# Clustering setup of a two-layer image kernel: loads issued in the stage before, entry ahead of the last stores, fewer and wider operations

## The chip, the cores and the metric

The kernel is one program on one core of a Trainium2 chip. The metric is the device time of one execution in microseconds (us). The runs of the kernel before took a median of 7005.86 us.

## What is computed

The input is x of shape (2, 96, 256, 256) in float32. Layer 0 adds to it a window attention followed by an MLP with a depthwise convolution, on the group-normalised x. Layer 1 adds a clustering step to the result, which is called x1 in the kernel:

```
x = x + L0(_gn(x))          # attention windows, fc1, 5x5 depthwise conv, fc2
x = x + L1(_gn(x))          # clustering
# L1, for y = _gn(x), 2 images, 4 heads of 24 channels, each image folded into 4 quarters
feat  = f_w y + f_b ;  value = v_w y + v_b
centres, value_centres = 2 x 2 average pooling of feat and of value, for each quarter
sim   = sigmoid(beta + alpha * <unit(centre), unit(feat)>), kept for the best centre alone
agg   = (sim @ value + value_centres) / (sum(sim) + 1)
out   = proj_w (agg @ sim) + proj_b
```

Because everything ahead of the similarity is linear in x once the group statistics are known, the kernel folds the normalisation, both projections, and the product with the centres into one weight matrix for each quarter, called `rhs` (97 rows: 96 channels and one row for the biases; 208 columns: feature, value and 16 dot products). The stage that builds it is the setup of the clustering.

## The kernel before, in words

The program is a row of stages, each a block of instruction streams, one stream for each engine, with a barrier of all engines at its end: statistics, attention, `fc1`, `conv`, `fc2`, `cluster_setup`, `cluster`. The change touches `fc2` and `cluster_setup`, and the call of both in `program`.

`fc2` is the second product of the MLP. It goes over 14 tiles of rows (2 halves each). SyncE and ScalarE issue its DMAs (SP and ACT queues): x tiles `f_xa` (L1346), convolution results `f_sa` and `f_sbb` (L1356, L1357) into two buffers each. TensorE multiplies (L1411, L1414), VectorE adds the product and the bias onto `f_xa` (L1431) and takes sums for the pooling (L1437), and ScalarE takes sums of squares (L1449). Each tile of x1 is then stored (L1368) on both queues, and both streams end with a wait until all stores have landed (L1391 on SyncE). GpSimd has no stream here.

`cluster_setup` begins when those waits are over. SyncE issues 18 small loads of weights and constants (L1561), GpSimd sets four tiles (L1565 to L1569), and TensorE waits for all 18 loads and for the folded sums. VectorE leads one chain: fold the sums (L1623, L1625), gather them with TensorE (L1585), statistics, a square root on ScalarE (L1575), the scaled weights `wfv` (L1648), means `xm` (L1651, after which `stage` is 4), centres (L1595 to L1661). Then it spreads the centres and the means by quarter and head: 32 times two operations of 4 columns, `ctr` (L1668) and `xmq` (L1669). TensorE multiplies them (L1601, L1606), and VectorE writes 8 times two parts of `rhs` (L1674, L1675) and four copies of `value_centres` (L1678). Every VectorE operation here is followed by a wait on its own semaphore, in the helper

```
def link(ins):
    n[0] += 1
    ins.then_inc(dch, 1)
    dve.wait_ge(dch, n[0])
```

`cluster` follows: its loads of x1 start (L1776, L1781), VectorE sets tiles (L1937 to L1939), and TensorE's products with `rhs` (L1821) begin.

Of the kernel before, what the change touches and what calls it, by code (L numbers as in the profile page):

```python
# [7 lines left out]
F32 = mybir.dt.float32  # L8
BF16 = mybir.dt.bfloat16
ALU = mybir.AluOpType  # L10
# [1296 lines left out]
def fc2(nc, p, xs, sdr, x1, tab):  # L1307
# [5 lines left out]
    with ExitStack() as ctx:  # L1313
# [13 lines left out]
        psum = ctx.enter_context(nc.psum_tensor("f2_ps", [128, 2 * CGRP, 512], F32))  # L1327
# [6 lines left out]
        block = ctx.enter_context(nc.Block())  # L1334
# [37 lines left out]
        def _(sp):  # L1372
# [17 lines left out]
            for u in range(XA):  # L1390
                sp.wait_ge(stored[u], 16 * XLOADS * len(range(u, NTILE, XA)))  # L1391
# [49 lines left out]
        def _(act):  # L1441
# [24 lines left out]
            for u in range(XA):  # L1466
                act.wait_ge(stored[u], 16 * XLOADS * len(range(u, NTILE, XA)))
# [3 lines left out]
NCTR = 4  # L1471
# [3 lines left out]
NFC = 2 * C + EM  # L1475

# [26 lines left out]
def cluster_setup(nc, p, tab, t):  # L1503


    with ExitStack() as ctx:
        def sb(name, shape, dt=F32):
            return ctx.enter_context(nc.sbuf_tensor("cs_" + name, shape, dt))

        NBK = 16  # L1510
        folded = sb("folded", [128, CGRP, NBK + 1])
        pick = sb("pick", [128, B, 32])
        bsum = sb("bsum", [C, B, NBK])
        stat = sb("stat", [C, 2, B])
        avg = sb("avg", [C, 2, B])
        sq = sb("sq", [C, B])
        sd = sb("sd", [C, B])
        eps = sb("eps", [C, 1])
        scale = sb("scale", [C + 1, B])
        shift = sb("shift", [C, B])  # L1520
        group = sb("group", [C, C])
        heads = sb("heads", [C, CH_HEADS])
        same = sb("same", [C, C])
        fv_t = sb("fv_t", [C, 2 * C])
        fv_b = sb("fv_b", [C + 1, 2 * C])
        f_col = sb("f_col", [C, 1])
        f_nat = sb("f_nat", [C, B, C + 1])
        alpha = sb("alpha", [C, 1])
        wfv = sb("wfv", [C + 1, B, 2 * C])
        xm = sb("xm", [C + 1, B, NBK])  # L1530
        xmq = sb("xmq", [C + 1, NREG, CH_HEADS, NCTR])
        cf = sb("cf", [C, B, NBK])
        cs = sb("cs", [C, B, NBK])
        cn = sb("cn", [C, B, NBK])
        ctr = sb("ctr", [C, NREG, CH_HEADS, NCTR])
        psum = ctx.enter_context(nc.psum_tensor("cs_ps", [128, 8, 512], F32))
        loaded = ctx.enter_context(nc.semaphore("cs_loaded"))
        ones_set = ctx.enter_context(nc.semaphore("cs_ones_set"))
# [5 lines left out]
        gathered = ctx.enter_context(nc.semaphore("cs_gathered"))  # L1544
        block = ctx.enter_context(nc.Block())
        loads = [(pick[:], p["k_pick"]), (group[:], p["k_group"]), (heads[:], p["k_heads"]), (same[:], p["k_same_head"]),
                 (fv_t[:, 0:C], p["f_wt"]), (fv_t[:, C:], p["v_wt"]),
                 (fv_b[C:C + 1, 0:C], p["f_b"].rearrange("(a c) -> a c", a=1)),
                 (fv_b[C:C + 1, C:], p["v_b"].rearrange("(a c) -> a c", a=1)),
                 (f_col[:], p["f_b"].rearrange("(c a) -> c a", a=1)),  # L1550
                 (f_nat[:, 0, 0:C], p["f_w"]), (f_nat[:, 1, 0:C], p["f_w"]),
                 (alpha[:], p["sim_alpha"].partition_broadcast(C)),
                 (t["beta"][:], p["sim_beta"].partition_broadcast(128)),
                 (t["eye"][:], p["k_eye"]), (t["proj"][:], p["proj_wt"]),
                 (t["proj_b"][:], p["proj_b"].rearrange("(c a) -> c a", a=1)), (t["own_channels"][:], p["k_own_channels"]),
                 (t["combine"][:], p["k_combine"])]

        @block.sync
        def _(sp):
            for to, of in loads:  # L1560
                sp.dma_start(to, of).then_inc(loaded, 16)  # L1561

        @block.gpsimd
        def _(pool):
            pool.memset(eps[:], 1e-5).then_inc(ones_set, 1)  # L1565
            pool.memset(scale[C:C + 1, :], 1.0).then_inc(ones_set, 1)
            pool.memset(xm[C:C + 1, :, :], 1.0).then_inc(ones_set, 1)
            pool.wait_ge(ones_set, 3)
            pool.memset(t["value_centres"][:], 0.0).then_inc(ones_set, 1)  # L1569

        @block.scalar
        def _(act):
            act.wait_ge(ones_set, 4)
            act.wait_ge(stage, 2)
            act.activation(sd[:], sq[:], ACT.Sqrt, bias=eps[:]).then_inc(ach, 1)  # L1575
            act.wait_ge(pch, 4)
            act.activation(cs[:].rearrange("p b n -> p (b n)"), psum[0:C, 4, 0:B * NBK], ACT.Sqrt).then_inc(ach, 1)

        @block.tensor
        def _(pe):  # L1580
            pe.wait_ge(loaded, 16 * len(loads))
# [29 lines left out]
        def _(dve):  # L1611
# [7 lines left out]
            def staged():  # L1619
                dve.sem_inc(stage, 1)  # L1620
# [24 lines left out]
            dve.wait_ge(loaded, 16 * len(loads))  # L1645
# [457 lines left out]
```

## Time and profile before

| what | us |
|---|---|
| median of 3 runs | 7005.86 (7005.22 to 7007.62) |
| the profiled execution, its own time | 6989.15 |
| its span, first to last instruction | 6987.4 |
| `fc2`, from its first load to the end of its stores | 5363.5 to about 6056.8 |
| `cluster_setup`, first instruction to the last VectorE copy | 6057.2 to 6103.1 |
| `cluster`, from its first load to the end | 6103.6 to 6987.4 |

Times inside the execution are counted from its first instruction. "Busy" is the time in which an engine had an instruction running; PEclk is the granted clock of TensorE as a share of its full 2.4 GHz; the DMA share is the mean busy share of the core's 16 DMA engines. The execution that was profiled was 16.7 us shorter than the median of the runs.

### The profile page before, as it was taken

What the parts mean: (1) busy time and instruction counts of PE and PEld (TensorE: products, weight loads), DVE (VectorE), ACT (ScalarE), POOL (GpSimd) and SP (SyncE); (2) the same over time, 40 slices, a digit from 0 to 9 for tenths busy, and PEclk for the clock granted to TensorE, in tenths of its full rate; (3) what the DMA queues carried; (4) which work ended last, traced back from release to release, by engine and by line L of the source; (5) the groups of instructions that cost most, each with busy time, mean ns of one, the idle gap of its engine ahead of it and who ended that gap; (6) DMA issues with size and microseconds to landing.
All of it is one profiled execution on the core that took longest, in us unless ns stands there. A gap on an engine that the chain in (4) does not pass through costs nothing. (4 is left out here: it accounts for less than half of the span.)

```text
span 6987.4 us, 135774 instructions
## 1 busy us (share of the span) xinstructions
PE 6017.8 (86%) x51768; PEld 3105.6 (44%) x51768; DVE 5212.7 (75%) x7712; ACT 3497.1 (50%) x5182; POOL 2290.2 (33%) x4091
## 2 busy tenths in 40 slices
PE   0885999999999999999999689989996776488885
PEld 0332555555555555555555233345553111186661
DVE  7695888888888888888888456558885554556664
ACT  0553666666666666666666366644442111154340
POOL 0343455555554555555554656600000000000000
PEclk9997999999999999999999899999998888799995
DMA  7786344444454444444442788788897999637665
GB/s 306 192 240 172 74 102 100 104 106 106 108 114 90 102 105 100 101 108 104 108 105 52 190 253 244 219 324 343 344 344 250 294 308 314 188 93 206 187 191 180
DMA packets 761666, 1252.65 MB, mean 179 GB/s; under 512 B 159364, under 2 KB 477828, under 8 KB 730948
## 3 DMA queue, kind: packets, MB, share of 16 engines
q1 hardware_dynamic: 700532, 1090.77, 55.6%
q10 hardware_dynamic: 53328, 102.85, 5.0%
q0 software_dynamic: 7168, 50.34, 2.1%
q8 instruction: 422, 6.91, 0.4%
q14 instruction: 216, 1.77, 0.1%
HBM read 680.81 MB, written 508.40 MB: 170 GB/s over the span
## 5 line engine op out<-in xcount | busy, mean ns | idle before, releaser
L801 DVE TENSOR_REDUCE at_mz<-at_ps 128x4 bf16<-128x1024 f32 x1444 | 1772.4, 1227 | 105.1 <-PE at_ps L720 79.2
L668 ACT ACTIVATE at_E<-at_ps 128x1024 f32<-128x1024 f32 x1444 | 1399.4, 1021 | 381.5 <-PE at_ps L732 367.0
L732 PE MATMUL at_ps<-at_qaug,at_k 32*128 32x256 f32 x11552 | 829.1, 401 | 23.9 <-DVE at_qaug L842 23.9
L743 PE MATMUL at_ps<-at_E,at_vaug 128*32 128x256 f32 x11552 | 773.6, 385 | 5.6
L1283 PE MATMUL cv_ps<-cv_yin,cv_band 128*128 128x384 f32 x2304 | 746.3, 486 | 26.2 <-DMA cv_yin<-y_mlp 26.2
L1303 DVE TENSOR_TENSOR cv_yin<-cv_gl,cv_yin 64x384 f32<-64x384 f32 x1152 | 637.4, 553 | 150.0 <-ACT cv_gl L1294 142.2
L732 PEld LDWEIGHTS at_ps<-at_qaug,at_k 32*128 32x128 f32 x11552 | 522.5, 184 | 494.0 <-issue 383.2
L590 POOL TENSOR_TENSOR at_share<-at_rden,t_share 128x8 f32<-128x8 f32 x722 | 147.8, 205 | 1445.1 <-DVE at_rden L812 1445.1
L1283 PEld LDWEIGHTS cv_ps<-cv_yin,cv_band 128*128 128x128 f32 x2304 | 436.6, 190 | 336.1 <-DMA cv_yin<-y_mlp 27.0
L720 PE MATMUL at_ps<-at_k,at_q 32*128 32x256 bf16 x5776 | 573.7, 274 | 8.9 <-DMA at_k<-at_packed 7.5
L1294 ACT ACTIVATE cv_gl<-cv_ps,cv_bias 128x384 f32<-128x384 f32 x576 | 335.1, 582 | 436.6 <-PE cv_ps L1283 436.6
L842 DVE TENSOR_TENSOR at_qaug<-at_ps,at_q 128x256 f32<-128x256 f32 x722 | 306.5, 424 | 271.4 <-PE at_ps L766 271.4
L750 PEld LDWEIGHTS at_ps<-t_wv,at_y 96*128 96x128 f32 x2888 | 376.7, 190 | 297.4 <-issue 297.4
L750 PE MATMUL at_ps<-t_wv,at_y 96*128 96x96 f32 x2888 | 495.1, 294 | 0.0
L1565 POOL MEMSET cs_eps<- 96x1 f32 x1 | 0.1, 96 | 1506.4 <-POOLq L1313 1506.4
L1431 DVE SCALAR_TENSOR_TENSOR f_xa<-f_ps,f_b,f_xa 128x256 f32<-128x256 f32 x384 | 226.8, 667 | 352.5 <-PE f_ps L1414 351.7
L676 ACT ACTIVATE at_xa<-at_ps,t_out_shift 96x448 f32<-96x448 f32 (+2 forms) x304 | 314.5, 1035 | 346.8 <-PE at_ps L759 346.8
L1821 PE MATMUL cl_ps<-c_rhs,cl_xu 97*128 97x208 f32 x2048 | 433.6, 367 | 44.7 <-DMA cl_xu<-x 38.3
L1411 PE MATMUL f_ps<-f_sa,f_wa 128*32 128x512 f32 (+1 forms) x1728 | 237.2, 621 | 246.4 <-DMA f_sbb<-s_mlp 245.1
L743 PEld LDWEIGHTS at_ps<-at_E,at_vaug 128*32 128x32 f32 x11552 | 312.9, 109 | 287.0 <-issue 170.4
L1821 PEld LDWEIGHTS cl_ps<-c_rhs,cl_xu 97*128 97x128 f32 x2048 | 383.8, 205 | 114.1 <-issue 67.2
L705 PE MATMUL at_ps<-at_y,t_wqk 97*128 97x512 f32 x608 | 349.7, 658 | 55.4 <-DVE at_k L846 42.7
(216 smaller groups left out, 9625.5 us busy)
## 6 DMA issues: line engine op xcount, KB each, us to landing
cv_yin<-y_mlp SPq DMA_DIRECT2D x48, 2340.0 KB, 14.8
s_mlp<-cv_yin SPq DMA_DIRECT2D x48, 2340.0 KB, 8.4
at_rows_in<-y_attention SPq DMA_DIRECT2D x76, 768.0 KB, 6.1
gn_xin<-in_x SPq DMA_DIRECT2D x16, 3072.0 KB, 23.2
ln_xin<-in_x SPq DMA_DIRECT2D x192, 256.0 KB, 7.4
y_attention<-ln_xin SPq DMA_DIRECT2D x192, 256.0 KB, 3.8
cl_xu<-x SPq DMA_DIRECT2D x128, 384.0 KB, 3.7
cl_xv<-x SPq DMA_DIRECT2D x64, 768.0 KB, 6.4
```

The lines of the kernel that those rows point to most:

```text
L668: act.activation(E[:, m % 2, 2 * p:2 * p + 2, :], psum[:, 2 + 2 * p:4 + 2 * p, :], ACT.Exp).then_inc(exp_done, 1)
L676: act.activation(xa[:, 0:rows, cols(c)].rearrange("p r c -> p c r"), lin_ps[0:C, 0:CC * rows].rearrange("p (c r) -> p c r", r=rows), ACT.I ...
L705: pe.matmul(lin_ps, t["wqk"][:], y[:, n % 2, CK * c:CK * c + CK], start=True, stop=True).then_inc(qk_done, 1)
L720: i = pe.matmul(psum[:, g, TOK * j:TOK * j + TOK], q_upper[rows, n % 2, tokens(w, 128 * j, 128)], k_upper[rows, n % 2, tokens(w)], start=T ...
L732: i = pe.matmul(psum[:, 2 + h, TOK * j:TOK * j + TOK], k[rows, n % 2, tokens(w, 128 * j, 128)], qaug[rows, m % 2, :], start=True, stop=True)
L743: i = pe.matmul(pv_ps[32 * h:32 * h + VC, 0:TOK], vaug[:, m % 2, z, h, :], E[:, m % 2, h, z * TOK:(z + 1) * TOK], start=(z == 0), stop=(z ...
L750: i = pe.matmul(lin_ps[:, j * C:(j + 1) * C], y[0:C, n % 2, tokens(w, 128 * j, 128)], t["wv"][:], start=True, stop=True)
L801: dve.tensor_reduce(mz[:, m % 2].rearrange("p j (h c) -> p h j c", c=32)[:, 2 * p:2 * p + 2, :, DQ], psum[:, 0:2, :].rearrange("p h (j n) ...
L1283: m = pe.matmul(psum[:, n % NB, 0:3 * RUN], band[:, s, c, a, :], yin[:, s, c, 3 * u:3 * u + 3, GAP * a:GAP * a + RUN], start=(a == 0), sto ...
L1294: act.activation(gl[:, n % NG, :], psum[:, n % NB, 0:3 * RUN], ACT.Gelu, bias=bias[:, n // PARTS:n // PARTS + 1]).then_inc(gl_done, 1)
L1303: i = dve.tensor_tensor(yc, gl[half_rows(f), n % NG, :].rearrange("p (t n) -> p t n", n=RUN), yc, ALU.add)
L1821: m = pe.matmul(psum[:, 2 * half + g // 2, 256 * (g % 2):256 * (g % 2) + NFC], xu[:, n % XS, 128 * tile:128 * tile + 128], t["rhs"][:, f * ...
```

## The change

`fc2` gets its SBUF tiles and its PSUM from outside, so that the tiles of the setup live beside its own. Its two waits for the stores are taken out and handed on as a list. GpSimd gets a stream in `fc2` that issues the 18 loads and the four memsets. In the setup SyncE waits for the stores instead. `xmq` and the first 192 columns of `rhs` are spread by GpSimd, by 8 and by 2 wide copies; `ctr` takes VectorE 8 wide operations with no wait between them; the last 16 columns of `rhs` take 2, and `value_centres` takes 2 copies on VectorE and 2 on ScalarE.

```diff
@@ fc2
-            for u in range(XA):
-                sp.wait_ge(stored[u], 16 * XLOADS * len(range(u, NTILE, XA)))
+        @block.gpsimd
+        def _(pool):
+            for to, of in setup_loads(p, t, s):
+                pool.dma_start(to, of).then_inc(s["loaded"], 16)
+            pool.memset(s["eps"][:], 1e-5).then_inc(s["ones_set"], 1)
+            pool.memset(s["scale"][C:C + 1, :], 1.0).then_inc(s["ones_set"], 1)
+            pool.memset(s["xm"][C:C + 1, :, :], 1.0).then_inc(s["ones_set"], 1)
+            pool.wait_ge(s["ones_set"], 3)
+            pool.memset(t["value_centres"][:], 0.0).then_inc(s["ones_set"], 1)
...
-            for u in range(XA):
-                act.wait_ge(stored[u], 16 * XLOADS * len(range(u, NTILE, XA)))
+    return [(stored[u], 16 * XLOADS * len(range(u, NTILE, XA))) for u in range(XA)]
@@ cluster_setup
         @block.sync
         def _(sp):
-            for to, of in loads:
-                sp.dma_start(to, of).then_inc(loaded, 16)
+            for arrived, count in x1_stored:
+                sp.wait_ge(arrived, count)
         @block.gpsimd
         def _(pool):
...
+            pool.wait_ge(stage, 4)
+            for q in range(NREG):
+                pool.tensor_copy(xmq[:, q].rearrange("p e (i j) -> p e i j", j=2),
+                                 quarters(xm, q).unsqueeze(1).to_broadcast([C + 1, CH_HEADS, 2, 2])).then_inc(spread_done, 1)
+            for b in range(B):
+                pool.tensor_copy(t["rhs"][:, 4 * b:4 * b + 4, 0:2 * C], wfv[:, b, :].unsqueeze(1).to_broadcast([C + 1, 4, 2 * C])).then_inc(spread_done, 1)
+            pool.wait_ge(spread_done, NREG + B)
...
+            act.wait_ge(pch, 5)
+            for j in range(2):
+                rows_j = slice(32 * j, 32 * j + EM)
+                act.activation(t["value_centres"][rows_j].rearrange("p f c -> p (f c)"), psum[rows_j, 6, 0:NREG // 2 * C], ACT.Copy).then_inc(ach, 1)
+            act.wait_ge(ach, 4)
...
+            pe.wait_ge(spread_done, NREG)
             for f in range(NREG // 2):
...
             for q in range(NREG):
...
-                for e in range(CH_HEADS):
-                    link(dve.tensor_scalar(ctr[:, q, e, :].rearrange("p (i j) -> p i j", j=2), quarters(cn), heads[:, e:e + 1], None, ALU.mult))
-                    link(dve.tensor_copy(xmq[:, q, e, :].rearrange("p (i j) -> p i j", j=2), quarters(xm)))
-            staged()
+                last = dve.tensor_tensor(ctr[:, q].rearrange("p e (i j) -> p e i j", j=2),
+                                         quarters(cn, q).unsqueeze(1).to_broadcast([C, CH_HEADS, 2, 2]),
+                                         heads[:].unsqueeze(2).unsqueeze(3).to_broadcast([C, CH_HEADS, 2, 2]), ALU.mult)
+            last.then_inc(stage, 1)
             dve.wait_ge(pch, 5)
-            for q in range(NREG):
-                b = q // 4
-                link(dve.tensor_copy(t["rhs"][:, q, 0:2 * C], wfv[:, b, :]))
-                link(dve.tensor_scalar(t["rhs"][:, q, 2 * C:], psum[0:C + 1, 5, q * EM:(q + 1) * EM], scale[:, b:b + 1], None, ALU.mult))
-            for j in range(4):
+            for b in range(B):
+                dve.tensor_scalar(t["rhs"][:, 4 * b:4 * b + 4, 2 * C:], psum[0:C + 1, 5, b * 4 * EM:(b + 1) * 4 * EM].rearrange("p (q n) -> p q n", n=EM),
+                                  scale[:, b:b + 1], None, ALU.mult).then_inc(dch, 1)
+            for j in range(2, 4):
                 rows_j = slice(32 * j, 32 * j + EM)
-                link(dve.tensor_copy(t["value_centres"][rows_j].rearrange("p f c -> p (f c)"), psum[rows_j, 6, 0:NREG // 2 * C]))
+                dve.tensor_copy(t["value_centres"][rows_j].rearrange("p f c -> p (f c)"), psum[rows_j, 6, 0:NREG // 2 * C]).then_inc(dch, 1)
+            dve.wait_ge(dch, n[0] + B + 2)
```

`setup_loads` returns the same 18 pairs of tile and tensor as the list in the setup before, 0.48 MB in all.

## Rows read from the trace of the kernel before

**Rows 1.** Stretches (start:end, length, busy time of each engine, clock, DMA, GB/s).
```profile
core 0: us, PE busy (x) PEld busy (x) DVE busy (x) ACT busy (x) POOL busy (x), PEclk, DMA share, GB/s
5354.00:6057.00 703.00, 438.15 (x3456) 69.23 (x3456) 337.92 (x471) 107.42 (x169) 0.00 (x0) 0.81 1.00 292
6057.20:6066.70 9.50, 0.00 (x0) 0.00 (x0) 3.00 (x2) 0.00 (x0) 0.67 (x4) 0.50 0.25 50
6107.00:6112.00 5.00, 4.39 (x14) 4.11 (x15) 0.56 (x1) 0.42 (x2) 0.00 (x0) 0.58 1.03 264
6108.00:6850.00 742.00, 642.50 (x6428) 505.15 (x6431) 471.38 (x765) 315.67 (x831) 23.97 (x47) 0.92 0.60 171
```

**Rows 2.** Who waited for whom in `fc2`: total us, times, longest.
```profile
PE f_ps L1411 <- DMA f_sbb<-s_mlp: 245.1, 14, 57.9
...
SPq L1391 <- DMA x<-f_xa: 4.6, 1, 4.6
```

**Rows 3.** Order of time at the seam: start, us, engine, line [idle before].
```profile
6045.68 6.47 SPq L1368 DMA_DIRECT2D x<-f_xa  x6
6045.69 6.52 ACTq L1368 DMA_DIRECT2D x<-f_xa  x6
6057.19 0.35 SPq L1561 DMA_DIRECT2D cs_pick<-in_k_pick  x1
...
6057.23 2.85 DVE L1623 TENSOR_REDUCE cs_folded<-sums 128x48 f32<-128x1536 f32 x1 [11.66 <-PEq L1313]
...
6060.00 0.23 DVE L1625 TENSOR_REDUCE cs_folded<-squares 128x3 f32<-128x84 f32 x1
...
6066.71 0.41 PE L1585 MATMUL cs_ps<-cs_folded,cs_pick 128*32 128x17 f32 x12 [28.21 <-DMA c_combine<-in_k_combine]
```

**Rows 4.** Order of time in the rest of the setup.
```profile
6069.48 1.28 ACT L1575 ACT_TABLE_LOAD   x1 [23.87 <-DVEq L1620]
...
6075.41 0.18 DVE L1651 TENSOR_SCALAR cs_xm<-cs_bsum 96x32 f32<-96x32 f32 x1
...
6078.47 0.19 DVE L1660 TENSOR_TENSOR cs_cn<-cs_cn,cs_cf 96x32 f32<-96x32 f32 x1
...
6078.96 0.23 DVE L1668 TENSOR_SCALAR cs_ctr<-cs_cn,cs_heads 96x4 f32<-96x4 f32 x1
6079.22 0.17 DVE L1669 COPY cs_xmq<-cs_xm 97x4 f32<-97x4 f32 x1
...
6093.91 0.92 PE L1601 MATMUL cs_ps<-cs_ctr,cs_f_nat 96*97 96x64 f32 x4 [16.30 <-DVEq L1620]
...
6094.76 1.48 PE L1606 MATMUL cs_ps<-cs_wfv,cs_xmq 97*16 97x96 f32 x32
6096.31 0.26 DVE L1674 COPY c_rhs<-cs_wfv 97x192 f32<-97x192 f32 x1 [2.51 <-PE cs_ps L1606]
6096.60 0.23 DVE L1675 TENSOR_SCALAR c_rhs<-cs_ps,cs_scale 97x16 f32<-97x16 f32 x1
...
6100.81 2.32 DVE L1678 COPY c_value_centres<-cs_ps 16x384 f32<-16x384 f32 x4
...
6107.61 1.22 PE L1812 MATMUL cl_ps<-cl_zero 128*128 128x256 f32 x2 [11.37 <-DVE cl_xu L1939]
```

**Rows 5.** Groups by line: count | busy us, mean ns of one | idle before.
```profile
L1431 DVE SCALAR_TENSOR_TENSOR f_xa<-f_ps,f_b,f_xa 128x256 f32<-128x256 f32 x15 | 8.8, 665 | 2.2 <-PE f_ps L1414 2.2
```

**Rows 6.** Groups by line and shape: copies on GpSimd and on ScalarE.
```profile
L582 POOL COPY at_y<-at_rows_in 96x512 f32<-96x512 f32 x304 | 334.1, 1101 | 12.2 <-DMA at_rows_in<-y_attention 12.2
...
L622 POOL COPY at_saved<-at_ot 128x64 f32<-128x64 f32 x272 | 66.6, 245 | 0.0
...
L95 POOL COPY gn_lines<-gn_taps 96x10 f32<-96x10 f32 x20 | 2.8, 187 | 10.1 <-DMA gn_taps<-in_dw_taps 10.1
...
L1914 ACT ACTIVATE cl_val<-cl_ps 128x384 f32<-128x384 f32 x251 | 121.8, 485 | 0.0
```

**Rows 7.** DMA in 6057.2 to 6066.7: all packets, then those of SyncE's queue.
```profile
DMA packets 1956, 0.48 MB, mean 50 GB/s; under 512 B 1700, under 2 KB 1956, under 8 KB 1956
...
q1 hardware_dynamic: 1956, 0.48, 24.6%
```

More of the change, by code:

```diff
@@ L1312, in fc2 @@
     XA = 3
-    with ExitStack() as ctx:
+    with ExitStack() as block_ctx:
         def sb(nm, shape, dt=F32):
@@ L1475 @@
 NFC = 2 * C + EM
+NBK = 16
 def cluster_constants():
@@ new lines, in setup_tables @@
+def setup_tables(nc, ctx):
+    shapes = {"folded": [128, CGRP, NBK + 1], "pick": [128, B, 32], "bsum": [C, B, NBK], "stat": [C, 2, B],
+              "avg": [C, 2, B], "sq": [C, B], "sd": [C, B], "eps": [C, 1],
+              "scale": [C + 1, B], "shift": [C, B], "group": [C, C], "heads": [C, CH_HEADS],
+              "same": [C, C], "fv_t": [C, 2 * C], "fv_b": [C + 1, 2 * C], "f_col": [C, 1],
+              "f_nat": [C, B, C + 1], "alpha": [C, 1], "wfv": [C + 1, B, 2 * C], "xm": [C + 1, B, NBK],
+              "xmq": [C + 1, NREG, CH_HEADS, NCTR], "cf": [C, B, NBK], "cs": [C, B, NBK], "cn": [C, B, NBK],
+              "ctr": [C, NREG, CH_HEADS, NCTR]}
+    s = {k: ctx.enter_context(nc.sbuf_tensor("cs_" + k, shape, F32)) for k, shape in shapes.items()}
+    s["psum"] = ctx.enter_context(nc.psum_tensor("cs_ps", [128, 8, 512], F32))
+    s["loaded"] = ctx.enter_context(nc.semaphore("cs_loaded"))
+    s["ones_set"] = ctx.enter_context(nc.semaphore("cs_ones_set"))
+    return s
@@ new lines, in cluster_setup @@
+def cluster_setup(nc, p, tab, t, s, x1_stored):
+    with ExitStack() as ctx:
+        folded = s["folded"]
+        pick = s["pick"]
+        bsum = s["bsum"]
+        stat = s["stat"]
+        avg = s["avg"]
+        sq = s["sq"]
+        sd = s["sd"]
+        eps = s["eps"]
+        scale = s["scale"]
+        shift = s["shift"]
+        group = s["group"]
+        heads = s["heads"]
+        same = s["same"]
+        fv_t = s["fv_t"]
+        fv_b = s["fv_b"]
+        f_col = s["f_col"]
+        f_nat = s["f_nat"]
+        alpha = s["alpha"]
+        wfv = s["wfv"]
+        xm = s["xm"]
+        xmq = s["xmq"]
+        cf = s["cf"]
+        cs = s["cs"]
+        cn = s["cn"]
+        ctr = s["ctr"]
+        psum = s["psum"]
+        loaded = s["loaded"]
+        ones_set = s["ones_set"]
@@ L1544, in cluster_setup @@
         gathered = ctx.enter_context(nc.semaphore("cs_gathered"))
+        spread_done = ctx.enter_context(nc.semaphore("cs_spread_done"))
         block = ctx.enter_context(nc.Block())
[L1546 to L1556, printed above, removed]
+        LOADED = 16 * len(setup_loads(p, t, s))
@@ L1644, in _ @@
             staged()
-            dve.wait_ge(loaded, 16 * len(loads))
+            dve.wait_ge(loaded, LOADED)
             dve.wait_ge(pch, 2)
@@ L2074, in program @@
         t = cluster_tables(nc, ctx)
-        fc2(nc, p, xs, sdr, x1, tab)
-        cluster_setup(nc, p, tab, t)
+        with ExitStack() as inner:
+            s = setup_tables(nc, inner)
+            x1_stored = fc2(nc, p, xs, sdr, x1, tab, t, s, inner)
+            cluster_setup(nc, p, tab, t, s, x1_stored)
         cluster(nc, x1, out, t)
```

63 lines of the change are left out of this document (19 added, 44 removed).

## The prediction

> **What bounds the kernel now.** I read the stretches first. In `fc2`, 703 us long, the DMA engines are at a share of 1.00 and TensorE is busy for 438 us, so the stage is bound by its transfers [rows 1]; the view of waits says the same: TensorE waited 245 us in 14 waits for `f_sbb` [rows 2]. In `cluster`, TensorE is busy 642 of 742 us at a mean clock of 0.92 [rows 1]. Between them lies the setup, where in turn one engine or one transfer works and all others wait; what is taken out of that chain comes off the end, as nothing else runs. The order of time then gives the chain, link by link. The last stores of x1 are issued from 6045.7 to 6052.2 on both queues, and the next stage's first instructions start at 6057.2 [rows 3]; the queue's own waits put 4.6 us of that down to the landing of the stores [rows 2]. VectorE folds the sums until 6060.23, and TensorE starts its gather only at 6066.71, released by the last of the loads [rows 3]. Then follow 12.25 us of chain up to 6078.96, 14.95 us of spreading until TensorE starts at 6093.91, 2.4 us of products, and 6.82 us of copies from 6096.31 to 6103.13; `cluster` has its first matmul 4.5 us later [rows 4].
>
> **The change part by part.** Each term is a piece of that chain.
>
> (A) The wait for the stores moves from the end of `fc2` into SyncE's stream of the setup. The barrier can then pass when the last stores are issued, at 6052.2, not when they have landed, 4.6 us later [rows 2, 3]. Nothing stands behind the wait on SyncE but the end of the setup. The stores land at about 6056.8 whatever the barrier does, and the shortened setup still ends at about 6073.8 (6103.1 less 4.6 and the gains of B, C and D), so the wait is hidden by the setup itself. It would cost something only if the setup shrank below 4.6 us. Gain: 4.6 us, and less only if another engine were late; VectorE's and ScalarE's work is over when the last stores are issued from 6045.7 on [rows 3].
>
> (B) The 18 loads leave the head of the setup. The gather can start when the folding is done, at 6060.23, plus the 0.1 us that a signal takes here; it started at 6066.71 [rows 3]. Gain: 6.4 us. What is late next is VectorE's fold itself. The four memsets go too, but nobody waited for them.
>
> (C) 64 linked operations between 6078.96 and 6093.91 become 8 on VectorE. Before, one of the first kind took 0.23 us and its successor started after 0.26, one of the second 0.17 [rows 4]. The new kind, a product of two tensors with 16 columns, is not in the trace; the nearest row is the product of 32 columns, 0.19 us [rows 4]. Linked, it would take 0.22 with the gap of 0.03. Unlinked operations of one kind start sooner than they last: 15 of L1431 were busy 8.8 us together, 0.59 each, while one lasts 0.665, so 0.08 overlaps [rows 5]. Bounds for one: 0.11 (0.19 less 0.08) and 0.26 (the pace of before). I take 0.2, near the nearest row, as four dimensions with broadcasts are untried: 1.6 us for 8, plus 0.1 for the signal. Gain: 14.95 - 1.7 = 13.2 us, between 12.8 and 13.9. The Trainium skill ("VectorE: DVE Perf Modes", section "The DRAIN you can't avoid") says that leaving out semaphores between VectorE operations gains nothing and that their number is what counts; by it the eight would take 8 x 0.22 = 1.8 us, and the sum would be 0.2 us smaller. The overlap of L1431 speaks against it [rows 5].
>
> The other half, `xmq`, goes to GpSimd, from the moment when `stage` is 4, at 6075.6 [rows 4]. A GpSimd copy of 10 columns took 0.187 us, one of 64 took 0.245 [rows 6]; 8 of 16 columns take about 0.2 each, 1.7 us, until 6077.3. TensorE needs them after its four products for the centres, on that clock at 6080.7 + 0.9 = 6081.6. They have 4.3 us to spare, so each could take 0.74 us before it costs. Nothing is charged.
>
> (D) The last copies. The first 192 columns of `rhs` go to GpSimd as 2 copies of 768 columns. Rates: 1101 ns for 512, or 2.15 ns a column, and 245 for 64 with a slope of 1.9 between the two [rows 6]; that is 1.6 us each, until 6080.6, while the end of the setup on this clock is at 6084.8. Hidden, with 4 us to spare. VectorE keeps 2 operations of 64 columns from PSUM, each 0.23 [rows 4] plus 48 more columns at about a nanosecond, 0.28, and 2 copies of 384 columns at 2.32/4 = 0.58 [rows 4]: 1.7 us. ScalarE does its 2 copies beside them, each 0.485 by its nearest row from PSUM [rows 6], about 1.0 us. 6.82 us become 1.7. Bounds: 1.4 if VectorE's overlap as L1431 does; 2.3 if ScalarE must load a table of 1.28 us first [rows 4]. Gain: 5.1 us, between 4.5 and 5.4.
>
> (E) The loads are not gone. They go out at the head of `fc2`, where the DMA engines are at 1.00 for the whole stage [rows 1], and a stage bound by its transfers gives nothing back. Their price is the time that they took of 16 engines: 24.6% of 9.5 us, 2.3 us, for 1956 packets, 1700 of them under 512 B [rows 7]. They now come from GpSimd's queue, whose small packets this trace does not show. Lower bound: nothing, if they fit in gaps. Upper bound: all of the 9.3 us that they lasted from first issue to TensorE's start [rows 3], if the first tiles of `fc2` must stand behind them. I take 2.3. GpSimd itself has no other work in `fc2` (busy 0.00) [rows 1], so the issue of 18 DMAs and the memsets costs nothing.
>
> Sum: 4.6 + 6.4 + 13.2 + 5.1 - 2.3 = 27.0 us. The chain of 12.25 us, the products of 2.4 and the 4.5 us of entry into `cluster` stay. The profiled execution would go from 6989.15 us, of which the span is 6987.4 and 1.75 lies around it, to 6962.1. The median of the runs is 16.7 us above that execution; nothing in the change scales, so I take the same difference from the median: 7005.9 - 27.0 = 6978.9 us, 0.39% less. A difference of less than 0.2%, or 14 us, is about what a measurement of this kernel can't tell from none.
>
> **The rivals.** (1) Engines in each other's way. GpSimd's two wide copies, 6077.3 to 6080.6, lie beside VectorE's products of two tensors (from 6078.96) [rows 4, 6]. If one holds up the other for their whole length, VectorE's eight operations end up to 3.3 us later: 6982.2 us. For it: the overlap is there, and nothing like it stands in the setup of before. Against it: none of the rows measures a hindrance. The Trainium skill ("GPSIMD Engine Reference", section "1. Specifications") says that GpSimd's SBUF interfaces are shared with VectorE and contended by VectorE instructions with two SBUF inputs, which the new ones are and the old ones, with a scalar for each partition, were not; by this rule the time is the one just given.
>
> (2) The loads cost `fc2` their whole 9.3 us, 7 more than charged: 6985.9 us. For it: TensorE's longest wait, 57.9 us, is at the head of the stage, exactly where they are put [rows 2]. Against it: they are 0.48 MB of a stage that moves 292 GB/s for 703 us.
>
> (3) The change does not do what it says: the barrier doesn't pass earlier, or TensorE's gather finds another wait, and A and B together (11.0 us) are lost: 6989.9 us. Against it: each other stream of `fc2` is done 6.5 us ahead. Together with rival 1 this comes within 0.2%, above 6992.
>
> (4) Slower. TensorE's clock is at 0.50 through the setup and full again within 5 us of the start of `cluster`: 0.58 in the stretch from 6107 to 6112 [rows 1]. The idle time ahead of that start shrinks by 29 us, so the clock's falls in `cluster` come at other places of the work. Where the mean there, 0.92 over 742 us, fell to c, the stage would take 742 x (0.92/c - 1) more if it were all TensorE's. To give back 27 us and 14 more, c must be at 0.87; at 0.86 it is +52 us, 7031 us. For it: TensorE is what fills that stage. Against it: the instructions and waits of `cluster` are the same, and the wait that ends the idle time ends as before.
>
> **How the numbers follow.** The forecast with its own bounds gets 0.62: from 4.6 + 6.4 + 13.9 + 5.4 = 30.3 us gained, with the loads at nothing, to 4.6 + 6.4 + 12.8 + 4.5 - 4.6 = 23.7, with the loads at twice their price, thus 6975.6 to 6982.2. Rival 1 gets 0.15 (6979 to 6983), rival 2 0.11, rival 3 0.05, rival 4 0.03, other 0.04. The time is that of the forecast, 6979. The range goes down to 6972, as the runs of before already spread by 2.4 us, and up to 6988, to take in rivals 1 and 2. Faster by over 0.2% is everything below 6992: the forecast, rivals 1 and 2 and most of 3, 0.90; within 0.2%: 0.07; slower: 0.03.
>
> **What would show it right or wrong.** After: TensorE's wait in front of the gather ends on VectorE, about 3.2 us after the setup's first instruction, not on a DMA (B). The first instruction of the setup comes about 0.3 us after the last issue of a store, with DMA still busy (A). Eight operations on `cs_ctr` in 1.6 us (C); GpSimd's last copy ends ahead of TensorE's L1606 products (C, D). From VectorE's first fold to the entry of `cluster` some 22 us, where it was 46. `fc2` from its first load to its last store issue 2 us longer (E); 9 longer is rival 2. A `cs_ctr` operation of over 0.4 us is rival 1; a clock below 0.90 in `cluster` is rival 4. The prediction is wrong if `fc2` grows by over 15 us, or if a wait of over 10 us stands in the new setup.

## The result

| what | us |
|---|---|
| the changed kernel, median of 4 runs | 6952.97 (6946.11 to 6956.04) |
| the kernel before beside it, median of 4 runs | 7005.54 (6985.80 to 7007.62) |
| ratio, 95% interval | 0.9932, 0.9915 to 0.9949 |
| the profiled execution after, its own time and span | 6952.65, 6950.9 |

The kernel became faster by 48 us (7005.54 less 0.9932 of it), with an interval of 36 to 60. Forecast were 27. The direction was right; the time lies 19 us below the lower end of the range, and the question is where the other 20 us come from.

The stretches of the profile after, which answer to [rows 1]:

```profile
core 0: us, PE busy (x) PEld busy (x) DVE busy (x) ACT busy (x) POOL busy (x), PEclk, DMA share, GB/s
5361.00:6036.00 675.00, 439.27 (x3456) 69.35 (x3456) 336.69 (x469) 106.84 (x168) 10.19 (x22) 0.82 1.01 300
6036.00:6057.20 21.20, 6.42 (x62) 4.40 (x62) 10.52 (x37) 2.73 (x5) 2.69 (x10) 0.50 0.14 52
6062.00:6804.00 742.00, 640.94 (x6291) 504.99 (x6290) 466.85 (x758) 315.33 (x831) 23.85 (x47) 0.92 0.60 170
```

The whole of `fc2` now fits in 675 us. TensorE, VectorE and ScalarE are busy in it for the same time as before; the DMA engines are again at a share of 1, but move 300 GB/s where they moved 292. The clustering has the clock of before, 0.92. The order of time, from the last stores of `fc2` to the first instruction of `cluster` (start, us, engine, line), which answers to [rows 3, 4]:

```profile
6028.98 6.15 SPq L1368 DMA_DIRECT2D x<-f_xa  x6
6028.99 6.20 ACTq L1368 DMA_DIRECT2D x<-f_xa  x6
...
6035.66 2.84 DVE L1661 TENSOR_REDUCE cs_folded<-sums 128x48 f32<-128x1536 f32 x1 [6.78 <-PEq L1313]
...
6038.42 0.23 DVE L1663 TENSOR_REDUCE cs_folded<-squares 128x3 f32<-128x84 f32 x1
...
6038.80 0.41 PE L1622 MATMUL cs_ps<-cs_folded,cs_pick 128*32 128x17 f32 x12 [16.99 <-DVE cs_folded L1663]
...
6047.79 1.15 POOL L1597 COPY cs_xmq<-cs_xm 97x16 f32<-97x16 f32 x8 [676.09 <-DVEq L1658]
...
6048.86 0.88 DVE L1693 TENSOR_TENSOR cs_cs<-cs_cf 96x32 f32<-96x32 f32 x1
6048.88 1.59 POOL L1600 COPY c_rhs<-cs_wfv 97x768 f32<-97x768 f32 x2
...
6051.73 0.77 DVE L1701 TENSOR_TENSOR cs_ctr<-cs_cn,cs_heads 96x16 f32<-96x16 f32 x8
...
6052.56 0.92 PE L1638 MATMUL cs_ps<-cs_ctr,cs_f_nat 96*97 96x64 f32 x4 [2.17 <-DVE cs_ctr L1701]
...
6054.95 0.99 ACT L1613 ACTIVATE c_value_centres<-cs_ps 16x384 f32<-16x384 f32 x2 [4.34 <-PE cs_ps L1644]
...
6054.95 0.47 DVE L1707 TENSOR_SCALAR c_rhs<-cs_ps,cs_scale 97x64 f32<-97x64 f32 x2 [2.45 <-PE cs_ps L1644]
...
6055.46 1.15 DVE L1711 COPY c_value_centres<-cs_ps 16x384 f32<-16x384 f32 x2
...
6057.11 0.32 SPq L1810 DMA_DIRECT2D cl_xu<-x  x1
6057.24 0.27 DVE L1971 MEMSET cl_zero<- 128x256 f32 x1 [0.63 <-PEq L1545]
```

From the fold to the first load of `cluster` it is 21.45 us (6035.66 to 6057.11); before it was 46.4 (6057.23 to about 6103.6). TensorE's gather is now released by VectorE's fold, 3.14 us after the fold begins, no longer by a load. The wait for the stores stands in the setup, on SyncE, and hides there (total us, times, longest):

```profile
SPq L1591 <- DMA x<-f_xa: 4.3, 1, 4.3
```

So the seam gave what was forecast. The surprise is in `fc2`: from its first load, at 5360.86, to the fold it is 674.8 us. Before it was 693.7 (5363.5 to 6057.23). That is 18.9 less, of which 4.8 are the wait for the stores. About 14 us of the stage have gone although nothing was taken out of it, and 18 loads were added. Between the two profiled executions the span fell by only 36.5 us (6987.4 to 6950.9): 2.6 ahead of `fc2`, 18.9 in it and 25.0 at the seam were won, and the clustering lasted 893.8 us where it had lasted 883.7. What its length is worth as evidence is taken up at the end.

### The profile page after: what moved, and what is told of

It is laid out like the page before. It is cut to its first block and busy times, and to the rows that moved or that the text cites. A ratio compares the mean times of both kernels' runs of the same rounds, so it can differ in the third digit from the quotient of the medians.

```text
span 6950.9 us, 135713 instructions
## 1 busy us (share of the span) xinstructions
PE 6022.4 (87%) x51768; PEld 3109.7 (45%) x51768; DVE 5197.1 (75%) x7640; ACT 3498.0 (50%) x5184; POOL 2304.1 (33%) x4119
## 5 line engine op out<-in xcount | busy, mean ns | idle before, releaser
L1855 PE MATMUL cl_ps<-c_rhs,cl_xu 97*128 97x208 f32 x2048 | 438.6, 370 | 48.3 <-DMA cl_xu<-x 40.8
L1439 DVE SCALAR_TENSOR_TENSOR f_xa<-cs_ps,f_b,f_xa 128x256 f32<-128x256 f32 x384 | 226.8, 667 | 338.5 <-PE cs_ps L1422 337.7
L1419 PE MATMUL cs_ps<-f_sa,f_wa 128*32 128x512 f32 (+1 forms) x1728 | 237.5, 622 | 231.2 <-DMA f_sbb<-s_mlp 229.9
L655 ACT ACTIVATE at_packed<-at_ps 128x512 f32<-128x512 f32 x304 | 181.6, 597 | 422.8 <-PE at_ps L705 412.0
```

Of the source, the lines that this page charges most:

```text
L1855: m = pe.matmul(psum[:, 2 * half + g // 2, 256 * (g % 2):256 * (g % 2) + NFC], xu[:, n % XS, 128 * tile:128 * tile + 128], t["rhs"][:, f * ...
```

## The experiments

Four theories stood at first; the expectations, which were written ahead of each run, give three of them by letters. **Place** (L, and in its later form L256, where the remainder counts, against D, where the distance counts): the SBUF tiles of the setup now lie below those of `fc2`, so that `f_sa`, `f_sbb` and `f_xa` begin 7104 bytes higher in each partition, and with other remainders against 256 bytes; transfers to and from them then run at another speed. **Seam**: stores, loads or barrier at the end of `fc2` gave more than was counted. **Queue** (Q): the loads on GpSimd's queue at the head of `fc2` shift the order of the other queues' transfers. **Scatter** (S): executions differ by that much, and nothing is to be explained. Times below are medians, with the ratio to the kernel before in the same job and its 95% interval, and the gain in us is worked out of the ratio with 7000 us.

**e1: the kernel before, unchanged.** No edit.

> The kernel before, unchanged, for a second profile of it. In the two profiles so far the stage fc2, from its first load to the fold of the setup, is 693.7 us before and about 674 us after, and the clustering stage is 883.8 and 893.8 us, though the change adds 0.48 MB of loads to the one and nothing to the other. If these are properties of one execution (theory S, scatter), the second profile of the kernel before has fc2 anywhere from 670 to 694 us. If they are properties of the program (theory L, the place of the tiles of fc2 in SBUF; or theory Q, the loads on GpSimd's queue), fc2 is again 692 to 695 us, and its time is within 5 us of 7005 or, as in one run, 6986.

Measured: 6988.94 beside 6998.28, ratio 0.9989 (0.9978 to 1.0000), and 693.7 us became 699.8 from the first load of `fc2` to the fold. The stage is 5 to 6 us longer than either theory allowed, so one program's `fc2` differs by 6 us between two profiles. The same program comes out 8 us apart in two submissions of one job. That is the scatter against which every single difference below has to be read, and the intervals of single ratios don't cover all of it; 20 us are more than it.

**e2: only the places of the tiles.** The setup's tiles and its PSUM are allocated ahead of `fc2`; loads, waits and operations stay as before. The diff is against the kernel before:

```diff
-        fc2(nc, p, xs, sdr, x1, tab)
-        cluster_setup(nc, p, tab, t)
+        with ExitStack() as inner:
+            s = setup_tables(nc, inner)
+            x1_stored = fc2(nc, p, xs, sdr, x1, tab, t, s, inner)
+            cluster_setup(nc, p, tab, t, s, x1_stored)
```

> The tables and the PSUM tile of the setup are allocated ahead of fc2 as in the changed kernel, so that the tiles of fc2 lie at the changed kernel's addresses; loads, waits and operations are those of before. Theory L (place of the tiles): fc2 is about 20 us shorter, and the whole is 15 to 22 us below before. Theory Q (the loads on GpSimd's queue at the head of fc2 shift the order of the other queues' transfers for good) and theory S (scatter): the time is before's within 3 us in the mean.

**e3: the seam alone** (terms A, B and E on the new places, the spreading as before; against the changed kernel):

```diff
-            pool.wait_ge(stage, 4)
-            for q in range(NREG):
-                pool.tensor_copy(xmq[:, q]...
+            pool.wait_ge(ones_set, 4)
...
-                last = dve.tensor_tensor(ctr[:, q]...
+                for e in range(CH_HEADS):
+                    link(dve.tensor_scalar(ctr[:, q, e, :]...
+                    link(dve.tensor_copy(xmq[:, q, e, :]...
```

> Terms A, B and E without C and D: loads and memsets in fc2, the wait for the stores in the setup, and the many small linked operations of before. By the terms: 4.6 + 6.4 - 2.3 = 8.7 us below before, 6997 us. Theory L and theory Q both: 20 us more, 29 us below. Theory S: 8.7, with the scatter of the runs around it.

**e4: the wide operations alone** (terms C and D on the new places; loads and waits as before; against the changed kernel):

```diff
-            for to, of in setup_loads(p, t, s):
-                pool.dma_start(to, of).then_inc(s["loaded"], 16)
+            for u in range(XA):
+                sp.wait_ge(stored[u], 16 * XLOADS * len(range(u, NTILE, XA)))
```

> Terms C and D alone, on the changed kernel's addresses: few wide operations on VectorE, GpSimd and ScalarE; loads and waits as before. By the terms: 13.2 + 5.1 = 18.3 us below before. The profile after shows the spreading in 0.8 us and the last copies in 1.7 us, with 0.7 us lost where a product of two tensors on VectorE took 0.88 us beside GpSimd's wide copy; so 18.5 us as measured. Theory L: 20 us more than that, 38 below before. Theory Q and theory S: 18 to 19 below before.

Measured, beside 6998.28 for the kernel before (fc2: first load to fold; seam: fold to first instruction of `cluster`):

| | median | ratio | gain, us | fc2 | seam |
|---|---|---|---|---|---|
| e2 places | 6977.77 | 0.9971 (0.9960 to 0.9982) | 20 (13 to 28) | 676.1 | 46.4 |
| e3 seam | 6971.31 | 0.9959 (0.9945 to 0.9974) | 29 (18 to 38) | 678.2 | 40.2 |
| e4 wide | 6958.81 | 0.9943 (0.9928 to 0.9957) | 40 (30 to 50) | 686.6 | 27.8 |

e2 does none of the change's work and yet takes 20 us, with the seam at 46.4 as before. e3 is 6.5 us below e2, e4 19.0 below e2; together 6977.8 - 6.5 - 19.0 = 6952.3, and the changed kernel measured 6953.0. The change is thus a sum of three parts, and the part that was not forecast is the one that only moves addresses (of SBUF and of PSUM; the pads below move SBUF alone). The theories of the seam and of the queue fall, as e2 has neither the new waits nor the loads on GpSimd's queue. The stage of e2 goes from 5364.60 to the fold:

```profile
5364.60 0.34 SPq L1373 DMA_DIRECT2D f_wa<-in_fc_w  x1
...
6040.67 2.85 DVE L1647 TENSOR_REDUCE cs_folded<-sums 128x48 f32<-128x1536 f32 x1 [11.51 <-PEq L1313]
```

The gather in e3:

```profile
6038.04 2.84 DVE L1649 TENSOR_REDUCE cs_folded<-sums 128x48 f32<-128x1536 f32 x1 [6.87 <-PEq L1313]
...
6041.18 0.41 PE L1611 MATMUL cs_ps<-cs_folded,cs_pick 128*32 128x17 f32 x12 [17.08 <-DVE cs_folded L1651]
```

3.14 us from the start of the fold, where it was 9.48 [rows 3]: term B is here, whole, and it doesn't need the wide operations.

**e5 and e6: the kernel before with its `fc2` tiles moved.** An unused tile ahead of `fc2`'s own moves all of them by 192 bytes (e5), or by 7168 (e6), which is about the distance of the change with every remainder against 256 left as it was.

```diff
+        sb("pad", [128, 48])        # e5: 192 bytes
+        sb("pad", [128, 1792])      # e6: 7168 bytes
```

> The kernel before with a tile of 192 bytes ahead of the tiles of fc2. The place of a tile in its partition's memory is a fact of the program: before, f_xa begins at byte 96832, which is 64 above a multiple of 256; in the changed kernel at 103936, a multiple of 256. Here it begins at 97024, a multiple of 256. Theory L256 (the place counts through its remainder to 256, as every transfer of f_xa is a row of 2048 bytes): fc2 is 15 to 24 us shorter than the 694 and 700 us of the two profiles of before, and the whole is 12 to 20 us below before, like the layout alone. Theory D (another property of the place, such as the distance from other tiles, counts): no change within 4 us. Apart from that: by the Trainium skill (DMA: Bandwidth & Descriptors, section on how a descriptor splits into AXI transactions) a transaction must start at a multiple of 256 bytes, so that rows of 2048 bytes that begin 64 above one take 9 transactions in place of 8.

> The kernel before with a tile of 7168 bytes (28 times 256) ahead of the tiles of fc2: they move about as far as in the changed kernel (7104), and every remainder to 256 stays that of before. Theory L256: no change, fc2 694 to 700 us, the whole within 4 us of before. Theory D: the gain of the layout, 12 to 20 us.

**e7: the changed kernel with its tiles moved by 64 bytes**, so that `f_xa` doesn't begin at a multiple of 256 again:

```diff
+        sb("pad", [128, 16])
```

> The changed kernel with a tile of 64 bytes ahead of the tiles of fc2, so that f_xa begins 64 above a multiple of 256 as before. Theory L256: what the change gains shrinks from 47 us to the 27 of the terms, 0.4% below before, and fc2 lasts about 690 us in place of 675. Theory D, and theory Q (the loads on GpSimd's queue): 45 to 50 us below before, as without the 64 bytes.

**e8: the changed kernel with `cl_xu` and `cl_xv` of `cluster` at multiples of 256** (they begin 96 bytes above one):

```diff
+        sb("pad", [128, 40])        # ahead of cl_xu
```

> The changed kernel with a tile of 160 bytes ahead of the tiles of the clustering, so that cl_xu and cl_xv, which lie 96 above a multiple of 256 in both kernels, begin at multiples of it. Theory L256: their transfers get shorter, and of TensorE's 38 to 41 us of waits for cl_xu some part goes: 3 to 15 us less than the changed kernel, 50 to 62 below before. If that stage is not bound by transfers at all: no change from the changed kernel, 47 below before.

Measured, beside 6995.27: e5 6983.83, 0.9983 (0.9971 to 0.9996); e6 6998.25, 1.0004 (0.9990 to 1.0017); e7 6969.49, 0.9965 (0.9951 to 0.9980); e8 6951.87, 0.9936 (0.9913 to 0.9958). The distance alone does nothing: e6 has it and is the kernel before in time. The remainder does: e5, which has no tile of the setup below it, gains 12 us, and e7 is 17.6 us above e8 in the same job, with one line added to the changed kernel. In the profile `fc2` lasts 675.1 us to the fold in e5 and 693.4 in e6; in e7 it lasts 703.0, where about 690 were expected. e8 shows nothing that can be told from the changed kernel, and the 3 to 15 us expected of it did not come: its 6951.87 is within the scatter of 6952.97. TensorE's wait for `cl_xu` was 34.6 us and not 40.8, but the unchanged program had 34.7 in its second profile (e9), so that is scatter too. `cluster` is not bound by its transfers (share 0.60).

**e9 to e12: the size of it, and the price of the loads.** e9 is the changed kernel again. e10 issues its 18 loads sixteen times, each round after the last has landed. e11 puts `f_sa` and `f_sbb` at multiples of 256 too, each of their rows lengthened to one. e12 moves the tiles of the kernel before by 64 bytes, so that `f_xa` begins 128 above a multiple.

```diff
+            for again in range(16):                                   # e10
+                for to, of in loads:
+                    pool.dma_start(to, of).then_inc(s["loaded"], 16)
+                pool.wait_ge(s["loaded"], 16 * len(loads) * (again + 1))
...
-        sa = sb("sa", [128, 2, 2, PHASES, LINE])                      # e11
-        sbb = sb("sbb", [128, 2, PHASES, LINE])
+        sb("pad", [128, 48])
+        sa = sb("sa", [128, 2, 2, PHASES, 704])
+        sbb = sb("sbb", [128, 2, PHASES, 704])
...
+        sb("pad", [128, 16])                                          # e12
```

> The changed kernel, unchanged, for a second profile and more runs: 47 us below before in the mean as in its first four runs if that was no luck of the draw; by the terms (27.0 and 0.7 less for the product beside GpSimd's copy) and the place of the tiles as the pad of 192 bytes gave it (11.5), 38 us. The seam, from the fold to the first memset of the clustering, is 21.5 us again. TensorE's idle time and the clustering stage: its 893.7 us, where three profiles with the tiles of before had 879 to 884, are either a property of the program, then again 890 to 898, or scatter, then anywhere from 879 to 898.

> The changed kernel with the 18 loads on GpSimd's queue issued 16 times over, each round after the last has landed, into the same tiles: 7.2 MB more. If the loads cost fc2 what they took of 16 engines (term E, 2.3 us a round), the whole is 15 x 2.3 = 35 us above the changed kernel. If they fit in gaps, it is within 4 us of it. If they cost as in the rival with 9.3 us for the first round, later ones may cost the same: 140 us.

> The changed kernel with a tile of 192 bytes ahead of f_sa and rows of 704 in place of 650 elements in f_sa and f_sbb, so that every row of f_sa and f_sbb begins at a multiple of 256 bytes, as those of f_xa do already. Theory L256 taken further: rows of 2592 and 2072 bytes that begin at multiples save a transaction in some cases; fc2 is 3 to 12 us shorter than the changed kernel's. If the far end of these rows in device memory, which lies at multiples of 520 bytes, sets their time: no change within 4 us.

> The kernel before with 64 bytes ahead of the tiles of fc2: f_xa begins 128 above a multiple of 256. Theory L256: as slow as before, fc2 693 to 700 us, packets of 2048 bytes at 94 to 95 ns in the mean. If a multiple of 128 is enough: like the pad of 192 bytes, fc2 675 us, packets at 89 to 91 ns, the whole 11 to 20 us below before.

Measured, beside 6999.35: e9 6949.05, 0.9927 (0.9914 to 0.9940), so the gain repeats. e10 6968.87, 0.9957 (0.9943 to 0.9971): 20.7 us above e9 for 15 more rounds, 1.4 us a round (6969.3 less 6948.6 in the means); by the stage, 692.9 less 675.8 over 15, it is 1.1. By term E it would have been 2.3 a round, if the loads fit in gaps nothing: it is a little over half of the former. e11 6956.41, 0.9940 (0.9922 to 0.9957): no gain in the runs, though `fc2` is the shortest of all, 671.9, 3 to 4 us below the changed kernel's. e12 6986.42, 0.9988 (0.9975 to 1.0001), with `fc2` at 692.7: 128 bytes above a multiple is as slow for the stage as 64. The queues in the first half of `fc2` of e10 (packets, MB, share of 16 engines):

```profile
q0 software_dynamic: 9216, 7.62, 9.1%
```

16 rounds are 9216 packets, 576 for one. The same 0.48 MB took 1956 packets on SyncE's queue [rows 7]. On GpSimd's queue the packets are fewer than the ones by which the loads were priced.

These later rounds don't stand at the head of the stage, where the one round of the changed kernel stands. The head can be read by itself, from the first load of `fc2` to TensorE's first product, before:

```profile
5363.54 0.35 SPq L1373 DMA_DIRECT2D f_wa<-in_fc_w  x1
...
5411.84 1.94 PE L1411 MATMUL f_ps<-f_sa,f_wa 128*32 128x512 f32 x8 [57.86 <-DMA f_sbb<-s_mlp]
```

and after:

```profile
5360.86 0.34 SPq L1373 DMA_DIRECT2D f_wa<-in_fc_w  x1
...
5410.66 1.94 PE L1419 MATMUL cs_ps<-f_sa,f_wa 128*32 128x512 f32 x8 [59.35 <-DMA f_sbb<-s_mlp]
```

In the nine profiles without the loads it is 46.8 to 48.3 us (mean 47.4), in the seven with one round 48.1 to 50.4 (mean 49.4): the loads hold up the head by 2.0 us.

**e13 to e15: which tile.** Until here `f_xa` and the other two had moved together. e13 moves only `f_xa` of the kernel before to a multiple of 256. e14 moves `f_sa` and `f_sbb` as e5 does and leaves `f_xa` 64 above one. e15 moves only `f_xa` of the changed kernel, to 64 above.

```diff
+        sb("pad_xa", [128, 48])     # e13, between f_sbb and f_xa
...
+        sb("pad", [128, 48])        # e14, ahead of f_sa
+        sb("pad_xa", [128, 16])     # e14, between f_sbb and f_xa
...
+        sb("pad_xa", [128, 16])     # e15, between f_sbb and f_xa
```

> The kernel before with 192 bytes between f_sbb and f_xa: f_xa begins at a multiple of 256, f_sa and f_sbb stay where they were. The pad of 192 bytes moved all three. Theory L256 with f_xa as its place: fc2 lasts 672 to 680 us, its packets of 2048 bytes take 89 to 91 ns in the mean, and the whole is 10 to 18 us below before. If it was f_sa or f_sbb that gained: fc2 692 to 700 us, packets at 94 to 95 ns, within 9 us of before (the second submission of the unchanged kernel was 8 us off the runs of before beside it).

> The kernel before with 192 bytes ahead of the tiles of fc2 and 64 more ahead of f_xa: f_sa and f_sbb lie as in the pad of 192 bytes, f_xa is again 64 above a multiple of 256. Theory L256 with f_xa as its place: fc2 692 to 700 us, packets at 94 to 95 ns. Otherwise: fc2 672 to 680 us and 10 to 18 us below before.

> The changed kernel with 64 bytes between f_sbb and f_xa, the mirror of the one before: f_xa alone loses its place. Theory L256 with f_xa as its place: fc2, from its first load to the fold, 15 to 25 us longer than the 675 and 676 us of the changed kernel, and the whole 15 to 25 us above it, about 25 to 32 below before. Otherwise: within 5 us of the changed kernel, 44 to 50 below before.

Measured, beside 6997.38: e13 6986.32, 0.9985 (0.9973 to 0.9996); e14 6985.35, 0.9983 (0.9973 to 0.9993); e15 6969.06, 0.9957 (0.9943 to 0.9970). On the side of the changed kernel the runs answer: e15 moves nothing but `f_xa` and is 16 us above the first result of the changed kernel and 20 above e9, as e7 was 16 and 20. On the side of the kernel before they don't: e13 and e14 are the same in time, though only one of them should have gained. The stage does tell them apart, if not by the expected lengths. e13:

```profile
5360.52 0.35 SPq L1374 DMA_DIRECT2D f_wa<-in_fc_w  x1
...
6043.54 2.85 DVE L1624 TENSOR_REDUCE cs_folded<-sums 128x48 f32<-128x1536 f32 x1 [11.80 <-PEq L1313]
```

and e14:

```profile
5362.55 0.34 SPq L1375 DMA_DIRECT2D f_wa<-in_fc_w  x1
...
6063.20 2.85 DVE L1625 TENSOR_REDUCE cs_folded<-sums 128x48 f32<-128x1536 f32 x1 [11.59 <-PEq L1313]
```

683.0 us against 700.6, with the same wait at the end. For e13 672 to 680 were expected. e15 lasts 686.5 to the fold, 11 to 12 us more than the changed kernel, where 15 to 25 were expected: the direction is the same each time, and the size of a single pair is within what two profiles of one program differ by.

All 17 profiles put together, with the wait for the stores left out (first load to the start of TensorE's last product with `f_sa`), and the mean length of the packets of 2048 bytes, which are the rows of `f_xa`, 47,600 of them in that stretch, worked out of the records of the packets. (The expectations speak of means over the middle of the stage; from 5420 to 6020 us they are 93.3 to 94.6 ns in the seven profiles off a multiple and 87.8 to 89.6 in the nine on one without e10.) Lengths stand in the order of the names:

| `f_xa` begins | loads in `fc2` | first load to last product, us | packet of 2048 B, mean ns |
|---|---|---|---|
| 64 or 128 above a multiple of 256 | no (before, e1, e6, e12, e14) | 673.3, 679.1, 672.9, 672.4, 680.3 | 95.8 to 97.8 |
| 64 above | yes (e7, e15) | 687.1, 670.6 | 96.7, 95.6 |
| at a multiple | no (e2, e4, e5, e13) | 655.8, 666.4, 654.9, 662.5 | 92.5 to 93.3 |
| at a multiple | yes (after, e3, e8, e9) | 659.2, 662.6, 664.7, 660.4 | 91.7 to 92.5 |
| at a multiple, the other tiles too | yes (e11) | 656.3 | 91.3 |
| at a multiple, loads 16 times | yes (e10) | 677.3 | 93.8 |

Without the loads the means are 675.6 and 659.9: 16 us; with one round (e11 left out) they are 678.9 and 661.7: 17 us. Apart from e10 the groups don't overlap, and the packets don't either. 47,600 packets that are 3.6 to 4.1 ns shorter in the mean, over 16 DMA engines, are 11 to 12 us (an estimate) of a stage in which those engines set the pace.

## Why the prediction was right, and where it failed

**What bounds the kernel.** Right: the stage was bound by its transfers [rows 1], the setup by its chain [rows 3, 4]. Each microsecond taken out of the chain came off the end.

**(A) The wait for the stores, 4.6.** Shown. From the start of TensorE's last product with `f_sa` to the fold it was 20.4 us and is 15.6: 4.8. The wait stands hidden on SyncE with 4.3 us, beside a setup of 21.

**(B) The loads off the head, 6.4.** Shown by e3: 9.48 us became 3.14, so 6.3; the seam went from 46.4 to 40.2.

**(C) The spreading, 13.2, bounds 12.8 to 13.9.** The mechanism was right, the size just beyond its bound: 14.95 us became 0.83, a gain of 14.1. Eight products took 0.77 us together, 0.1 each, where 0.11 was the lower end and 0.2 was taken: each lasts 0.164 us and begins 0.09 after the one before it. What misled was the nearest row, 32 columns in 0.19 us, which was one operation that others waited for. By the Trainium skill ("VectorE: DVE Perf Modes", section "The DRAIN you can't avoid") leaving the semaphores out saves nothing between VectorE operations. Here the trace speaks against it: unlinked, the operations follow each other at 0.1 us, linked ones of a quarter of the columns followed at 0.26 [rows 4]. The same section adds that a next operation that isn't held starts earlier, and that is what the eight do. No run linked the eight, so how much of the pace is the missing link and how much the kind of operation was not measured. GpSimd's eight copies took 1.15 us (1.7 forecast), well ahead of their use at 6053.40.

**(D) The last copies, 5.1.** Shown: 6.82 became 1.66, thus 5.2. GpSimd's two wide copies took 1.59 us together, where 1.6 each had been reckoned from copies of [rows 6].

**Rival 1, engines in each other's way.** The mechanism is there, at another place and for a fifth of its price. Because GpSimd was done with its small copies sooner, its wide ones began at 6048.88, beside VectorE's square of `cf` and not beside `ctr`. That operation, 96 x 32, took 0.88 us. In e3, where GpSimd copies nothing (tile view: count, shortest/median/longest in ns, first and last start):

```profile
L1681 DVE TENSOR_TENSOR cs_cs<-cs_cf x1: 186/186/186, 6051.2 to 6051.2; 96x32 f32<-96x32 f32 x1
```

and in e4, where it does:

```profile
6060.69 1.14 POOL L1596 COPY cs_xmq<-cs_xm 97x16 f32<-97x16 f32 x8 [17.65 <-DVEq L1657]
...
6061.76 0.88 DVE L1692 TENSOR_TENSOR cs_cs<-cs_cf 96x32 f32<-96x32 f32 x1
6061.77 1.60 POOL L1599 COPY c_rhs<-cs_wfv 97x768 f32<-97x768 f32 x2
```

0.7 us are lost on the chain: VectorE's operation lasts until 0.04 us after the end of the first of the two copies, which takes 0.82 us (6048.88 to 6049.70 after, with VectorE done at 6049.74). So it was held up for the whole length of one copy. The rule of the Trainium skill that the prediction cited for this rival ("GPSIMD Engine Reference", "1. Specifications") holds for this operation, which reads two operands from SBUF.

The seam as a whole: 46.4 us forecast to lose 24.7 (B, C and D) lost 25.0.

**(E) The loads, 2.3.** Right in kind and nearly in size: 2.0 us at the head of the stage, by TensorE's first product; the stage as a whole is 1.8 us longer with them (661.7 and 659.9, at a multiple). A further round later in the stage costs 1.1 to 1.4 us (e10). That it is cheap because it is 576 packets and not 1956 was not tested. Rival 2, 9.3 us at the head, is excluded by those 2.0; its form in which each round costs as much fails by e10 too, where fifteen more would have cost 140.

**Rival 3** did not happen, as A and B are there. **Rival 4** was not seen: the clock in the clustering is 0.92 after as before.

**The step that failed** is in the part on the change, where the places of the tiles have no term at all. The change was described as giving `fc2` "its SBUF tiles and its PSUM from outside" (in the program `fc2` still allocates its tiles, but behind those of the setup, which is what moves them), and (E) then took it that "a stage bound by its transfers gives nothing back". It gave 16 us back. Moving `f_xa` from 64 bytes above a multiple of 256 to a multiple makes each of its transfers shorter, and in this stage nothing hides that. The sum as measured: 4.8 (A) + 25.0 (B to D) - 2.0 (E) + 16 (place) = 43.8 us, beside 48 in the first job and 51 in the second (0.9932 and 0.9927). With `f_xa` moved off its multiple, e7 and e15 gain 24.5 and 30 us (0.9965 and 0.9957): on average 27, which is the forecast, though either interval is some 20 us wide (14 to 34 and 21 to 40). The failure is thus one missing term, not one wrong one; that the terms B to D as measured come out so near their forecast together has a little luck in it, since C gave 0.9 more and the 0.7 of rival 1 took it back.

The rule that would have given it is also in the Trainium skill ("DMA: Bandwidth & Descriptors", section "How a descriptor splits into AXI transactions"): a descriptor is cut at 256-byte boundaries, so that 2048 bytes are 8 pieces when they begin on one and 9 when they don't. It agrees in sign, in that 64 and 128 above are alike (e12), and in that the distance is without effect (e6). In size the section leaves two readings, both estimates from its figures: 9 pieces for 8 are 12.5%, while by its count of 32-byte beats, where the unused bytes ahead of the start are fetched as well, 66 for 64 are 3%. The packets' mean rose by 4% (96.5 against 92.9 ns without the loads), which is near the second and far from the first. The medians of the packets are the same, 84 ns, and the upper quarter begins at 96 to 101 ns off a multiple and at 84 to 87 on one, so it is the longer ones that grew. Which of the two readings makes them longer was not tested.

**What stays open.** On the side of the kernel before, the runs show less of it than the stage: aligned, e2, e5 and e13 gained 20, 12 and 10 us, but e1, e12 and e14, which are not, also 8, 8 and 12, and e6 lost 3. The mean of the three is 14, of the four 6. The profiles are one execution each, the runs scatter by 8 us from submission to submission, and the length of the clustering itself went from 879 to 898 us over the profiles, in no order that any edit explains. Without the change's loads its mean was 893.5 us in the four aligned profiles and 886.5 in the five others, which takes 7 of the 16 us back; with the loads there is no such difference (889.0 and 890.8), and no run shows whether the 7 are more than scatter. That `f_xa`'s place shortens `fc2` is shown by the profiles, in which the groups don't overlap; that it is worth 16 to 20 us in the runs is shown for the changed kernel (e7, e15); for the kernel before the runs give no more than the 8 us between those means, with an uncertainty as large. Why `f_sa` and `f_sbb` (packets of 2592 bytes, 154 to 163 ns with no pattern) gain nothing that the runs show was not settled.

None of the versions beats the changed kernel: e8, e9 and e11 are within 4 us of it.

## What to carry to other kernels

A change that moves the allocation of a stage moves the start address of its tiles, and where the stage is bound by its transfers that is an edit of its own: list the tiles' addresses against 256 bytes before and after, and give them a term. An unused tile of a few bytes tests it, and the stage's own length in the profile shows it sooner than the whole time does.

Work taken out of a serial chain is worth its own length, as A to D show to within a microsecond of their forecasts; to price operations that nobody waits for, don't take the row of one that is waited for.

Where a result is better than the forecast, it has a cause as well: the test is a kernel that has none of the change's work (e2), and one that has all of it but the suspected side effect (e7, e15).

## What the runs showed of the hardware

- A tile's start address matters for DMA: rows of 2048 bytes that begin at a multiple of 256 took 91 to 93 ns in the mean over the stage (94 with the loads 16 times), others 96 to 98, under a load of all 16 engines; the stage was 16 us of 676 shorter.
- Small loads on GpSimd's queue were 576 packets, on SyncE's 1956, for the same 0.48 MB; in a stage that had no free DMA time one round cost 2.0 us at its head and each further one 1.1 to 1.4.
- VectorE products of 96 x 16 that no one waits for one by one follow at 0.1 us, each lasting 0.164; linked to each other, operations of 4 columns followed at 0.26 (other operations, so not the link alone).
- One VectorE operation with two inputs in SBUF went from 0.19 to 0.88 us beside a GpSimd copy of 97 x 768, and ended 0.04 us after that copy, which took 0.82 us itself.
